# Scores, maxima and turned maxima of two stacked attentions: one wide matrix product each, or four over 32 array columns

## The reference

```python
# layer 0: two softmaxes, over 257 image rows and over the text rows, added
scores = jnp.einsum('bqhd,bkhd->bhqk', q, k) * scale
probs = jax.nn.softmax(scores, axis=-1)
return jnp.einsum('bhqk,bkhd->bqhd', probs, v)
# layer 1: keys and values are the context itself, the last 256 keys masked causally
scores = jnp.einsum('bhqd,bhkd->bhqk', qh, kh) / math.sqrt(hd)
scores = jnp.where(causal[None, None], scores, MASKED_BIAS)
out = jnp.einsum('bhqk,bhkd->bhqd', jax.nn.softmax(scores, axis=-1), vh)
```

## Time and profile before

| | |
|---|---|
| three runs, median (lowest to highest) | 1932.79 us (1930.95 to 1938.36) |
| profiled execution: its time | 1929.12 us |
| profiled execution: its span | 1927.1 us |
| PE products, weight loads | 12374 each |
| PE busy | 1745.1 us (91%) |
| DVE busy | 1274.9 us (66%) |
| ACT busy | 858.6 us (45%) |
| granted TensorE clock, mean | 0.957 |

### The profile page before, as it was taken

One profiled execution on the slowest core, in us unless ns is written; L12 is line 12 of the kernel. 1 busy time (PEld: TensorE's weight loads), 2 busy tenths in 40 slices (PEclk: granted clock), 3 DMA queues, 4 the chain that ended last, 5 costly groups with the idle time before them and its releaser, 6 DMA issues.

```text
span 1927.1 us, 32757 instructions
## 1 busy us (share of the span) xinstructions
PE 1745.1 (91%) x12374; PEld 1132.1 (59%) x12374; DVE 1274.9 (66%) x2850; ACT 858.6 (45%) x1404; POOL 558.4 (29%) x951
## 2 busy tenths in 40 slices
PE   5999999999877899899899989997888889999988
PEld 4888888888765445455454445664454444444447
DVE  6767666675656777777778543434345688888844
ACT  3333433333342265645646722442232456666652
POOL 5543444443223140320501012441111222331230
PEclk9999999999989799999999979998897999999999
DMA  3100010110006447245264185654602156754100
GB/s 111 33 12 12 23 33 2 33 57 12 18 1 123 92 111 115 40 99 81 45 136 61 17 269 190 215 175 111 137 1 47 31 77 145 88 95 69 23 1 22
DMA packets 91480, 142.74 MB, mean 74 GB/s; under 512 B 14566, under 2 KB 59819, under 8 KB 91324
## 3 DMA queue, kind: packets, MB, share of 16 engines
q1 hardware_dynamic: 86924, 127.79, 31.5%
q10 hardware_dynamic: 2528, 7.74, 1.3%
q0 software_dynamic: 1872, 5.13, 0.7%
HBM read 109.68 MB, written 32.03 MB: 74 GB/s over the span
## 4 chain that ended last, share of the span: by engine, by line
PE 68%; DVE 16%; issue 5%; ACT 5%; POOL 4%; DMA 1%; SPq 0%; ACTq 0%; DVEq 0%; POOLq 0%
PE bank L1237 9%; PE bank L1195 9%; PE bank L1214 7%; PE bank L1975 5%; PE bank L1547 5%; PE bank L777 3%; PE bank L1994 3%; PE bank L1861 3%; PE bank L1863 2%; PE bank L1862 2%; DVE xa_part_max L1310 2%; PE bank L2437 2%; PE bank L2422 2%; PE bank L742 1%; DVE da_neg L2556 1%
## 5 line engine op out<-in xcount | busy, mean ns | idle before, releaser
L1310 DVE TENSOR_REDUCE xa_part_max<-bank 128x1 f32<-128x448 f32 (+1 forms) x512 | 270.0, 568 | 36.3 <-PE bank L1195 33.1
L1271 ACT ACTIVATE xa_e<-bank 128x1024 f32<-128x1024 f32 (+1 forms) x208 | 212.7, 1023 | 136.0 <-PE bank L1214 134.0
L1271 ACT ACTIVATE ca_e<-bank 128x1024 f32<-128x1024 f32 (+2 forms) x208 | 196.4, 956 | 86.9 <-PE bank L1214 86.1
L1310 DVE TENSOR_REDUCE shared<-bank 128x1 f32<-128x400 f32 (+1 forms) x384 | 206.7, 570 | 33.6 <-PE bank L1195 29.8
L1195 PE MATMUL bank<-xa_kst,xa_qst 122*128 122x448 bf16 (+1 forms) x512 | 164.2, 354 | 13.3 <-DVE xa_part_max L1310 9.1
L1237 PE MATMUL bank<-xa_e,xa_vaug 128*17 128x256 f32 (+1 forms) x1664 | 130.8, 386 | 1.6 <-ACT xa_e L1271 0.6
L981 POOL TENSOR_TENSOR gsa_qk<-gsa_qk,gsa_rot 128x512 f32<-128x512 f32 x64 | 81.9, 1279 | 163.1 <-DVE gsa_rot L897 163.1
L1547 PE MATMUL bank<-xa_wkv,shared 128*128 128x256 f32 (+1 forms) x448 | 120.5, 398 | 8.0 <-SPq L281 3.5
L1237 PE MATMUL bank<-ca_e,ca_vaug 128*17 128x256 f32 (+2 forms) x1664 | 124.6, 372 | 3.2 <-POOL ca_e L1382 1.4
L1214 PE MATMUL bank<-xa_qst,xa_kst 128*128 128x256 bf16 (+1 forms) x832 | 126.7, 275 | 0.0
L1195 PEld LDWEIGHTS bank<-xa_kst,xa_qst 122*128 122x128 bf16 x512 | 45.6, 98 | 108.8 <-DVE xa_part_max L1310 63.8
(11 more groups left out here) (408 smaller groups left out, 4222.0 us busy)
## 6 DMA issues: line engine op xcount, KB each, us to landing
xa_kst<-xa_k_parts SPq DMA_DIRECT2D x96, 200.1 KB, 8.2
ca_kst<-ca_k_parts SPq DMA_DIRECT2D x96, 200.1 KB, 8.2
xa_k_parts<-xa_parts SPq DMA_DIRECT2D x8, 1200.8 KB, 6.9
ca_k_parts<-moe_ctx_parts SPq DMA_DIRECT2D x8, 1200.8 KB, 5.6
moe_gu<-in_expert_gate_up SPq DMA_DIRECT2D x8, 1024.0 KB, 14.2
shared<-in_ctxT_split ACTq DMA_DIRECT2D x4, 1601.0 KB, 9.5
moe_ctxT<-in_ctxT SPq DMA_DIRECT2D x8, 800.5 KB, 8.0
ca_cv<-in_ctx SPq DMA_DIRECT2D x4, 1536.0 KB
```

What stands on the lines that cost most here:

```text
L1271: e.activation(self.e[m % 3][0:rows, :, first:T], banks[m % 2][0:rows].rearrange("p a (h t) -> p (a h) t", t=T)[:, :, first:T], ACT.Exp, s ...
L1310: e.tensor_reduce(top, work[:, 0:hi - lo], AX.X, ALU.max).then_inc(*reduced(t, *step))
```

## The change

A new function `in_columns` makes a product in pieces of 32 weight columns (the last piece may be narrower), each into its own 32 partitions of the output, with the same moving operand. Scores and maxima go through it: one product of 128 columns becomes four of 32; one of 65 (the last key tile of ca, and one tile of xa) becomes three. The turned maxima were a transpose with a bfloat16 result; they become a product with the identity as the moving operand and a float32 result, which ACT reads in its place. With 24 or 12 columns they stay one product. Only the last piece of a product signals.

```diff
+        def in_columns(e, out, weights, rhs, start=True, stop=True):
+
+            n = out.shape[0]
+            for c in range(0, n, 32):
+                some = slice(c, min(c + 32, n))
+                mm = e.matmul(out[some], weights[:, some], rhs, start=start, stop=stop, skip_group_check=True)
+            return mm
...
-                    e.matmul(work[:, 0:hi - lo], qb[0:self.AUG, h_, i * P:(i + 1) * P], kb[0:self.AUG, h_, lo:hi], start=True, stop=True).then_inc(*mx_mm(t, *step))
+                    in_columns(e, work[:, 0:hi - lo], qb[0:self.AUG, h_, i * P:(i + 1) * P], kb[0:self.AUG, h_, lo:hi]).then_inc(*mx_mm(t, *step))
...
-                    S, psb = self.sets, work.bitcast(BF16)
+                    rows = self.sets * 3 * UNIT
...
-                        m = e.transpose(psb[0:S * 3 * UNIT, i * P:(i + 1) * P], self.neg[:, i, 0:S].rearrange("p s q h -> p (s q h)"), ident_bf[:])
+                        m = in_columns(e, work[0:rows, i * P:(i + 1) * P], self.neg[:, i, 0:self.sets].rearrange("p s q h -> p (s q h)"), ident_bf[:])
...
-                        mm = e.matmul(o, kb[:, j, k0:k0 + rows], qb[:, j, first:T], start=True, stop=True)
+                        mm = in_columns(e, o, kb[:, j, k0:k0 + rows], qb[:, j, first:T])
...
-                    e.copy(self.negT[n % 2][0:rows], work.bitcast(BF16)[0:rows, 0:T].rearrange("p (i t) -> p i t", i=TB)).then_inc(*neg_turned(t, *step))
+                    e.copy(self.negT[n % 2][0:rows], work[0:rows, 0:T].rearrange("p (i t) -> p i t", i=TB)).then_inc(*neg_turned(t, *step))
```

## The result

The changed kernel takes 1989.94 us (median of four runs, 1985.32 to 1997.16), the kernel before on the same chip 1931.87 (four runs, 1929.67 to 1938.36): a ratio of 1.0298, 95% interval 1.0255 to 1.0342. Forecast were 1902 us and a range of 1883 to 1930. The profiled execution took 1986.58 us, and its mean granted clock was 0.942 (0.957 before).

A forecast was written before the change was run, and what follows sets the result against it. PE was taken to lead, DVE a few per cent behind. 450 width changes x 0.10 = 45 us, 30 kept, other main terms 0: 1929.1 to 1899, runs' median 3.7 higher, 1903, said as 1902 us; range 1883 to 1930.

The forecast's parts named there:

- the one on instructions: PE in both attentions: denser instructions and 62 more packets of 1.2 us each stay hidden; taken as 0.
- the bound above, 74 us: PE's instruction queue: cost if each of the 62 added packets were waited for 1.2 us.
- Widths: PE in xa and ca: 450 changes between wide and narrow products removed, at 0.10 us each, 45 us of PE time.
- Pieces and loads: PE's scores and maxima: four pieces run side by side and their loads hide behind streaming; both taken as 0.
- What of it reaches the end: Whole kernel, stage by stage: of the 45 us of PE time saved, 30 us shorten the run.
- That DVE is what takes them: In ca: DVE with the maxima is late next, its share of 1600 to 1840 us rising from 84% to about 90%.
- Rival 2: PE in both attentions: slower, the stream of pieces can't be kept up; 2135 us, mildest 1950; chance 0.14.
- Idle PE inside a score step: PE's score products: a sign that, if seen, would make the forecast wrong; no size given.

The follow-up runs named there:

- run 5: The changed kernel with as many stack transfers, but each bringing only its first 64 columns from the fifth unit of each attention on; 1915.12 us, ratio 0.9937.
- run 1: The changed kernel with each unit's stack transfers spread by waits for PE's score tiles, from the fifth unit of each attention on; 1923.73 us, ratio 0.9994.
- run 12: The kernel before with pieces in ca and units 11 to 14 of xa, stack and feed-forward weight transfers spread over score tiles; 1910.05 us, ratio 0.9906.
- run 3: The changed kernel with only scores and turned maxima in pieces, the maxima products whole as in the kernel before; 2008.68 us, ratio 1.042.
- run 7: The kernel before with 12 always-met waits behind each wide product of both attentions, 16,128 more PE instructions, no pieces; 3003.1 us, ratio 1.5587.

## Why the prediction was wrong

**The step that failed** is the one on instructions: "256 instructions at 20 ns last 5 us: hidden, or 62 x 1.2 = 74 us if each were waited for. I take 0." The rate and the count were right. What was wrong is the 1.2 us: that is how long a packet takes once it moves, from a mean over the kernel. How long it waits until it moves was not asked. In a burst that is an estimated 7 us in the kernel before (the packet at 1707.43) and 9 in the longest stretch of the changed one. There it was covered, since 256 instructions at one in 53 ns last 13.6 us; at 20 ns they last 5, and PE stood still for 59.8 us in all. The packets' starts could have been read from the trace of before. The DMA share of such a burst is hidden in the mean of 0.33 to 0.65 of the earlier trace rows; by itself it is 1.1. That the bound above, 74 us, is near the 59.8 is luck: it is not 62 packets waited for 1.2 us each, but 23 waits, of up to 7.4 us.

The Trainium skill, Runtime: NRT & Kernel Launch, section Instruction fetch mechanics, says that the sequencer streams its program in blocks of 256 instructions and that the cost is "mostly hidden". The blocks agree, 161 packets of 16,384 bytes for some 41,400 PE instructions in the trace. Hidden they were here only where no burst of transfers was under way, or where 256 instructions lasted long enough (13.6 us).

**The second cost, not named at all**, is the clock. The prediction took PE's products at the full clock all along. The changed kernel and the one with thin transfers run the same program of PE, and PE is busy 1730.4 us in the one and 1710.8 in the other, at a mean clock of 0.942 and 0.954. Their spans differ by 73.9 us: 19.6 are this, 54.3 are idle time of PE. (The profiled executions; run 5's is 2.7 us under its median.)

**Widths** were right. I cut PE's program into runs of products of one kind and took for each run the time to the next run's start. By the medians of such runs in ca, value products to wide maxima were 559 ns and are 435 in the kernel with thin transfers; a 400 column maxima product to value products 265, now 174; four whole scores 438, now 439 in 16 pieces. Over the same stretch of ca, some 620 instructions of DVE long, the least time of its kind for each such run adds up to this, with what the runs took above it beside it (the two columns leave out the stretch's edges, some 2 us; how runs are grouped moves single sums by up to 6 us):

```
ca stage          length us   sum of least   above least
before               288.0        267.3         18.4
changed              320.8        242.8         75.5
spread (run 1)       278.1        236.1         39.5
thin (run 5)         272.5        238.4         31.6
```

300 changes of width fewer in ca at 0.10 us were to be 30 us, and the sum of the least times falls by 25 to 31. Pieces and loads cost nothing, as taken: 16 score pieces take the time of four whole scores.

**What of it reaches the end** was forecast as 30 us, and is 12 in run 5 (1915.12 against 1926.86) and 15.5 in run 12. This term too was taken too large. Part of it is the clock again: run 5's ten executions were granted 0.953 on average, the kernel before beside them 0.957, and over the executions of the kernel before 0.01 of clock goes with an estimated 13 to 15 us (1919.24 us at 0.963, 1936.64 at 0.951). That makes some 6 us of the missing 18 in run 5. In ca run 5 gains 15.5 us of 30 (288.0 to 272.5), where I had kept 20: what is above the least times rises by 13, with DVE busy 235.92 of 273 us (86%; it was 84%). That DVE is what takes them, as forecast, fits this share but is not shown by a run. In xa it should have been 10 to 12 and was some 3 by 1082 us, as the pieces gained nothing before 1000; the stretch of 6.9 us at 1103 then took it away. Why they gained nothing there is open.

**Rivals.** Rival 2 named the right side, a stream of pieces that can't be kept up, but saw the limit in the rate of pieces, which is kept up everywhere between the stretches, and priced it at 1950 or 2135; the measured 1989.94 lies between the two, by another mechanism. I gave the slower side 0.14, since the rows spoke for each piece's rate; no rival had the store of instructions and the burst as its mechanism. "Idle PE inside a score step" was named as what would make the forecast wrong, and it is what the profile shows.

## What to carry to other kernels

Cutting a product into pieces over columns cost nothing for each piece here, as long as the next 256 instructions arrived in time. Before such a change, look for the fullest stretches of DMA in the stage, count PE's instructions from one instruction packet to the next there, and turn what is above 256 into time at the old rate: that is how late the packet was (here up to 171 instructions at 53 ns, an estimated 9 us). In the changed kernel's ca PE stood still wherever the count reached 458 or more, some 200 above 256, and at the new rate of 20 ns those last only 4 us. Where the packets are later than that, spread the transfers over the work with waits on its progress; here that was worth some 60 us of 1990 to the cut kernel and nothing to the uncut one. And cut only where it removes changes of width: half a cut (run 3) was worse than the whole and than none.

## What the runs showed of the hardware

- An instruction packet can be late by an estimated 7 to 9 us, in the kernel before as in the changed one, when a burst of transfers fills the DMA engines: between two starts in ca lie up to 16.9 us in the changed kernel, with thin transfers 3.7 to 8.8. PE executed at most 549 instructions from one start to the next, 458 to 493 across nine of the eleven stretches in ca (the other two follow a packet that was late already), and went on 1.3 to 1.8 us after the packet had landed. With 443 or fewer, the kernel before never stood still.
- A change between products of 128 columns and of at most 32 costs 0.09 to 0.12 us each way, also between bfloat16 products: in run 3 16 score pieces take 553 ns to a whole maxima product (438 before, all whole), and a whole maxima product of 400 columns 272 to score pieces (180 before; medians).
- Four bfloat16 pieces of 32 columns and 256 moving columns with their loads take 0.110 us, as long as the one product of 128 (439 ns for 16 pieces, 438 for four whole products).
- Six instructions of PE that only wait on a semaphore already met cost 66 ns each behind a product, at a mean granted clock of 0.728 (run 7).
- The executions of one kernel differ with their mean granted clock: the kernel before took 1919.37 us at 0.963, 1925.7 at 0.957 and 1936.86 at 0.951.
